# A gated feed-forward stage: its products in two scaled float16 parts, and a store for each batch

## The reference, cut to what matters

```python
x = x + tanh(g_xattn[0]) * L0_xattn(layernorm(x), ctx_2048, mask)      # stage A
x = x + tanh(g_ffn[0])   * L0_ffn(layernorm(x), w_up, w_down)          # stage B
x = x + tanh(g_xattn[1]) * L1_xattn(layernorm(x), ctx_2048)            # stage C
x = x + tanh(g_ffn[1])   * L1_ffn(layernorm(x), w1, w2, w3)            # stage D
# L1_ffn, x: float32 [4, 512, 512], w1, w2: [1408, 512], w3: [512, 1408]
w1, w2, w3 = nf4_roundtrip(w1), nf4_roundtrip(w2), nf4_roundtrip(w3)
a = einsum('bsd,fd->bsf', x, w1)
b = einsum('bsd,fd->bsf', x, w2)
h = silu(a) * b
return einsum('bsf,df->bsd', h, w3)
```

## Time and profile before

| | us |
|---|---|
| median of 3 runs | 1945.01 (1943.62 to 1948.37) |
| profiled execution | 1953.13 |
| its span, first to last instruction | 1951.3 |
| TensorE busy in the span | 1709.4 |
| VectorE busy | 1279.7 |
| ScalarE busy | 788.8 |
| GpSimd busy | 849.4 |

### The profile page before, as it was taken

The page is one execution under the profiler, slowest core; times in us unless marked ns, Lnnn a source line. Parts: engine busy times, 40 slices in busy tenths (PEclk is TensorE's granted clock), DMA queues, the critical chain, the costliest instruction groups (busy, mean ns, idle before and its releaser), DMA issues. The chain is left out here.

```text
span 1951.3 us, 24011 instructions
## 1 busy us (share of the span) xinstructions
PE 1709.4 (88%) x8134; PEld 863.4 (44%) x8134; DVE 1279.7 (66%) x1681; ACT 788.8 (40%) x1291; POOL 849.4 (44%) x383
## 2 busy tenths in 40 slices
PE   5999999993566767999999999999999967989996
PEld 2444444442444544444444444444444324434443
DVE  3668989856987776776766766666766113455453
ACT  1111212112455541566666665666666543111010
POOL 0022222112543434587778776778877740000000
PEclk9999999996888875999999999999999886999998
DMA  8031212302000016244444444444443020000002
GB/s 326 8 103 35 68 68 68 127 30 88 1 1 0 0 49 148 56 107 107 106 107 107 107 107 108 107 107 107 99 98 85 1 89 1 1 0 0 0 0 86
DMA packets 83552, 137.20 MB, mean 70 GB/s; under 512 B 16606, under 2 KB 53490, under 8 KB 82678
## 3 DMA queue, kind: packets, MB, share of 16 engines
q1 hardware_dynamic: 83446, 135.84, 25.4%
HBM read 70.73 MB, written 8.66 MB: 41 GB/s over the span
## 5 line engine op out<-in xcount | busy, mean ns | idle before, releaser
L1261 DVE TENSOR_REDUCE c_piece_max<-c_unit 128x1 f32<-128x804 f32 x512 | 485.2, 985 | 238.8 <-PE c_unit L1399 236.1
L1357 ACT ACTIVATE c_prob<-c_scores 128x512 f32<-128x512 f32 (+1 forms) x832 | 473.8, 597 | 270.4 <-PE c_scores L1416 257.3
L1196 POOL TENSOR_TENSOR c_prob_sum<-c_prob_sum,c_prob 128x2048 f32<-128x2048 f32 x96 | 439.5, 4578 | 13.2 <-ACT c_prob L1357 7.4
L1416 PE MATMUL c_scores<-c_queries,c_keys 98*128 98x512 f32 (+1 forms) x832 | 356.7, 445 | 30.6 <-ACT c_prob L1357 15.5
L1399 PE MATMUL c_unit<-c_khigh,c_qdiag 128*128 128x402 f32 x1024 | 304.4, 382 | 22.3 <-DMA c_qdiag<-c_qhigh 11.2
L1399 PEld LDWEIGHTS c_unit<-c_khigh,c_qdiag 128*128 128x128 f32 x1024 | 187.7, 199 | 153.3 <-DVE c_piece_max L1261 92.2
L1416 PEld LDWEIGHTS c_scores<-c_queries,c_keys 98*128 98x128 f32 (+1 forms) x832 | 153.3, 187 | 199.8 <-ACT c_prob L1357 136.8
L1425 PE MATMUL c_out<-c_prob,c_VT 128*32 128x512 f32 (+1 forms) x1664 | 222.3, 614 | 0.0
L525 PE MATMUL a_S<-a_ctxT,a_xnT 128*128 128x401 f32 x512 | 188.8, 513 | 7.2 <-ACT a_prob L490 3.9
L555 PE MATMUL a_o<-a_ctx,a_probT 128*128 128x512 f32 (+1 forms) x416 | 181.2, 592 | 0.0
L1713 PE MATMUL d_o<-d_w3T,d_h 128*128 128x512 bf16 x528 | 126.7, 392 | 12.3 <-DVE d_h L1620 12.3
(11 more groups left out here) (203 smaller groups left out, 2126.6 us busy)
## 6 DMA issues: line engine op xcount, KB each, us to landing
c_keys<-c_khigh SPq DMA_DIRECT2D x128, 200.2 KB, 3.0
c_k<-in_keys SPq DMA_DIRECT2D x16, 801.0 KB, 6.0
c_keys<-c_k SPq DMA_DIRECT2D x64, 200.2 KB, 3.0
a_ctx<-in_ctx SPq DMA_DIRECT2D x12, 1024.0 KB, 5.5
c_VT<-in_values SPq DMA_DIRECT2D x16, 768.0 KB
a_ctxT<-in_ctxT SPq DMA_DIRECT2D x12, 802.0 KB, 4.8
c_queries<-c_qhigh SPq DMA_DIRECT2D x128, 64.0 KB, 2.7
a_weights<-in_L_ffn_weight SPq DMA_DIRECT2D x3, 1408.0 KB, 13.5
```

The costliest lines, as they stand in the source:

```text
L1196: nc.gpsimd.tensor_tensor(psum4[:], a[:], prob[(j * MC + c) % RING][:], ALU.add).then_inc(sums_taken, 2 if i == 1 else 1)
L1261: nc.vector.tensor_reduce(piece_max[j % 2][:, k // 2, k % 2:k % 2 + 1], U[bank(unit)][:, :, 0:PIECE], axis=AX.XY, op=ALU.max).then_inc(uni ...
L1357: nc.scalar.activation(prob[(j * MC + c) % RING][0:w, h, :], STp[h % 2][0:w, :], ACT.Exp, scale=SCALE).then_inc(exp_done, 1)
L1416: nc.tensor.matmul(STp[h % 2][0:w, :], K[p][:, h, c * P:c * P + w].bitcast(F32R), Q[p][:, h, :].bitcast(F32R), start=True, stop=True).then ...
```

## The change

The hidden products are multiplied by a scale and cut into two float16 parts instead of three bfloat16 parts. The multiplication by the scale goes into the instruction that multiplies silu by the second product. The scale is found at run time from the largest absolute weight: two reductions over the loaded weights, a transpose of the result on TensorE, a reduction, a small matmul that spreads the two values over all partitions, and a few small operations that give the scale and a gate divided by it. The down projection has two matmuls for each tile instead of three, and the addition to x uses the new gate. The four stores leave the fifth block, which is gone, and go into stage D's SyncE stream: each waits for the four additions of its batch.

```diff
+        hids = [sb(f"d_hid{j}", [P, S]) for j in range(3)]
+        hp = [sb(f"d_h{n}", [P, FC, S], F16) for n in ("hi", "lo")]
-        hid = sb("d_hid", [P, S])
-        hrest = sb("d_hrest", [P, S])
-        hp = [sb(f"d_h{n}", [P, FC, S], BF16) for n in range(3)]
+        HALF_RANGE = 2.0 ** 14
...
             for k in range(3):
                 sp.dma_start(wr[k][:], weights_dram[k]).then_inc(w_loaded[k], 16)
+            for b in range(B):
+                sp.wait_ge(x_added, ST + (b + 1) * ST)
+                sp.dma_start(out_dram[b].rearrange("(t p) d -> p t d", p=P), X[:, b * ST:(b + 1) * ST, :]).then_inc(stored, 16)
+            sp.wait_ge(stored, 16 * B)
...
             pool.memset(nhalf[:], -0.5).then_inc(consts_ready, 1)
-            pool.wait_ge(consts_ready, 1)
+            pool.memset(ones2[:], 1.0).then_inc(consts_ready, 1)
+            pool.wait_ge(consts_ready, 2)
...
-                nc.vector.tensor_tensor(hid[:], silu[f % 2][:], U[slot(ST + f)][:, 1, :], ALU.mult).then_inc(unit_read, 1)
+                hid = hids[f % 2 if f < FC - 1 else 2]
+                nc.vector.scalar_tensor_tensor(hid[:], silu[f % 2][:], hscale[:], U[slot(ST + f)][:, 1, :], ALU.mult, ALU.mult).then_inc(unit_read, 1)
                 dve.wait_ge(unit_read, 2 + n + 1)
                 steps.link(nc.vector.tensor_copy(hp[0][:, f, :], hid[:]))
-                steps.link(nc.vector.tensor_tensor(hrest[:], hid[:], hp[0][:, f, :], ALU.subtract))
-                steps.link(nc.vector.tensor_copy(hp[1][:, f, :], hrest[:]))
-                nc.vector.tensor_tensor(hp[2][:, f, :], hrest[:], hp[1][:, f, :], ALU.subtract).then_inc(h_ready, 1)
+                nc.vector.tensor_tensor(hp[1][:, f, :], hid[:], hp[0][:, f, :], ALU.subtract).then_inc(h_ready, 1)
                 steps.close()
 
+            def hidden_scale():
+                steps = Steps(dve, scale_steps)
+                for k in range(2):
+                    dve.wait_ge(w_loaded[k], 16)
+                    nc.vector.tensor_reduce(wmax[:, k:k + 1], wr[k][:], axis=AX.X, op=ALU.max, apply_absolute_value=True).then_inc(wmax_ready, 1)
+                dve.wait_ge(wmax_turned, 1)
+                steps.link(nc.vector.tensor_reduce(wtop[:], O[0][0:2, 0:P], axis=AX.X, op=ALU.max))
+                dve.wait_ge(consts_ready, 2)
+                nc.vector.tensor_scalar(wdiag[:], ident[0:2, 0:2], wtop[:], None, ALU.mult).then_inc(wdiag_ready, 1)
+
+            def hidden_scale_spread():
+                steps = Steps(dve, scale_steps, 1, 1)
+                dve.wait_ge(wtops_spread, 1)
+                steps.link(nc.vector.tensor_copy(wtops[:], O[1][:, 0:2]))
+                steps.link(nc.vector.tensor_tensor(hbound[:, 0:1], wtops[:, 0:1], wtops[:, 1:2], ALU.mult))
+                steps.link(nc.vector.tensor_scalar(hbound[:, 1:2], hbound[:, 0:1], float(D) * D / HALF_RANGE, 1e-30, ALU.mult, ALU.max))
+                steps.did(nc.vector.reciprocal(hscale[:], hbound[:, 1:2]))
+                steps.did(nc.vector.tensor_scalar(hgate[:], hbound[:, 1:2], gates[:, 3:4], None, ALU.mult))
+                steps.settle()
+
             layernorm(0)
+            hidden_scale()
             rest_of_x(0)
+            hidden_scale_spread()
...
-                    nc.vector.scalar_tensor_tensor(x, O[t][:], gates[:, 3:4], x, ALU.mult, ALU.add).then_inc(x_added, 1)
+                    nc.vector.scalar_tensor_tensor(x, O[t][:], hgate[:], x, ALU.mult, ALU.add).then_inc(x_added, 1)
...
+            pe.wait_ge(wmax_ready, 2)
+            nc.tensor.transpose(O[0][0:2, 0:P], wmax[:], ident[:]).then_inc(wmax_turned, 1)
             turn_x(0)
+            pe.wait_ge(wdiag_ready, 1)
+            nc.tensor.matmul(O[1][:, 0:2], ones2[:], wdiag[:], start=True, stop=True).then_inc(wtops_spread, 1)
             up(0, 0)
...
-                        for part in range(3):
+                        for part in range(2):
                             last = nc.tensor.matmul(O[t][:], hp[part][:, f, t * P:(t + 1) * P], w3T[:, f, :],
-                                                    start=f == 0 and part == 0, stop=f == FC - 1 and part == 2)
+                                                    start=f == 0 and part == 0, stop=f == FC - 1 and part == 1)
...
-            ffn_1(nc, shared, weights)
-        with nc.Block() as block:
-            @block.sync
-            def _(sp):
-                for b in range(B):
-                    sp.dma_start(out[b].rearrange("(t p) d -> p t d", p=P), X[:, b * ST:(b + 1) * ST, :]).then_inc(stored, 16)
-                sp.wait_ge(stored, 16 * B)
+            ffn_1(nc, shared, weights, out)
```

More of the change, by code:

```diff
@@ L1498, in _, with ffn_1 @@
             every_slot(pe, slot)
-def ffn_1(nc, shared, weights_dram):
+def ffn_1(nc, shared, weights_dram, out_dram):
     X, ident, ident_bf, gates = shared["X"], shared["ident"], shared["ident_bf"], shared["gates"]
@@ L1531, in ffn_1 @@
         silu = [sb(f"d_silu{j}", [P, S]) for j in range(2)]
-        hid = sb("d_hid", [P, S])
-        hrest = sb("d_hrest", [P, S])
-        hp = [sb(f"d_h{n}", [P, FC, S], BF16) for n in range(3)]
+        hids = [sb(f"d_hid{j}", [P, S]) for j in range(3)]
+        hp = [sb(f"d_h{n}", [P, FC, S], F16) for n in ("hi", "lo")]
+        HALF_RANGE = 2.0 ** 14
+        wmax = sb("d_wmax", [P, 2])
+        wtop = sb("d_wtop", [2, 1])
+        wdiag = sb("d_wdiag", [2, 2])
+        ones2 = sb("d_ones", [2, P])
+        wtops = sb("d_wtops", [P, 2])
+        hbound = sb("d_hbound", [P, 2])
+        hscale = sb("d_hscale", [P, 1])
+        hgate = sb("d_hgate", [P, 1])
         U = [ps(f"d_u{j}", [P, 2, 512]) for j in range(2)]
@@ L1549, in ffn_1 @@
         x_added = sem("d_x_added")
+        stored = sem("d_stored")
+        wmax_ready = sem("d_wmax_ready")
+        wmax_turned = sem("d_wmax_turned")
+        wdiag_ready = sem("d_wdiag_ready")
+        wtops_spread = sem("d_wtops_spread")
+        scale_steps = sem("d_scale_steps")
         ln_steps = sem("d_ln_steps")
@@ L1553, in ffn_1 @@
         UNITS = ST + FC
-        LN_STEPS, H_STEPS = ST + MOMENTS, 3
+        LN_STEPS, H_STEPS = ST + MOMENTS, 1
         tiles = [FC, FC, DC]
@@ L1730, in sem @@
             return stack.enter_context(nc.semaphore(name))
-        gates_loaded, gates_ready, ident_ready, id_steps, weights_stored, stored = (
-            sem(n) for n in ("gates_loaded", "gates_ready", "ident_ready", "ident_steps", "weights_stored", "stored"))
+        gates_loaded, gates_ready, ident_ready, id_steps, weights_stored = (
+            sem(n) for n in ("gates_loaded", "gates_ready", "ident_ready", "ident_steps", "weights_stored"))
         shared = dict(X=X, ident=ident, ident_bf=ident_bf, gates=gates, gates_ready=gates_ready, ident_ready=ident_ready,
```

## The result

| | before | after |
|---|---|---|
| median | 1946.69 us (4 runs, 1943.62 to 1948.71) | 1898.42 us (4 runs, 1896.57 to 1902.01) |
| profiled execution | 1953.13 us | 1898.57 us |
| its span | 1951.3 us | 1896.7 us |
| stage D, from the issue of its weight loads to the end | 354.0 us | 299.6 us |

The ratio is 0.9756, with a 95% interval of 0.9735 to 0.9777, which is a gain of 43 to 52 us. The medians differ by 48.3 us, and 48.8 was the predicted sum. As a time, 1896.2 us was forecast and 1898.4 measured; for the profiled execution 1904.3 was forecast and 1898.6 measured. The two profiles differ by more than the medians, 54.6 us, nearly all of it in stage D: its weight loads are issued at 1597.30 us before and at 1597.15 after. Why they differ by more than the medians is the main question that the experiments had to answer.

What follows compares the result with a forecast made beforehand. Stage D was taken as TensorE-bound batches plus a bare tail of stores. TensorE and VectorE 40.9, stores 8.2, scale -0.3 sum to 48.8 us, taking the median 1945.01 to 1896.2 us, range 1892 to 1901.

Steps and rivals of the forecast that it cites:

- The removed matmuls: Stage D down projection: 176 matmuls go, 168 of them on the path at 0.2158 us, 36.3 us gained.
- Rival D: Down matmuls: float16 stationary with bfloat16 moving runs at float32's rate, 90 us more, time 1986; chance 0.02.
- Rival E: Stage D: VectorE becomes the bound, little more than the stores' 8.2 us gained, time 1936; chance 0.01.
- The product chain: VectorE, each group: 1.19 us shorter, 1.86 stays; gains 2.2 before down(0), 1.0 before down(1), 1.4 at the end.
- the wait before down(1): TensorE waiting while layernorm(b+1) stands between hidden(0) and hidden(1): 3.17 us becomes 2.84, 0.33 gained three times.
- Where x is turned: Batch turn: the first cast on ScalarE decides, so these 4.7 us stay, nothing gained or lost.
- The scale: Start of stage D: reductions hidden beside weight loads and transposes, one small transpose on the path; -0.3 us, bounds 0 and -2.
- The stores: End of kernel: 5.3 us follow the last additions instead of 13.5, 8.2 us gained, bounds 4.8 and 8.6.
- Rival B: Tail: the last store lands no quicker than the median one, 45.4 us gained in all, time 1899.6; chance 0.07.
- The clock: TensorE at half clock behind waits: the 7.3 us of losses stay, change 0, bounds +7.3 and -7.
- Rival C: TensorE: 2.84 us of waiting spares the clock, which no longer falls; 56.1 us gained, time 1888.9; chance 0.07.
- rival A: TensorE: the clock falls more often, each fall dear; 42.3 us gained in all, time 1902.7; chance 0.11.

Runs made afterwards that it cites:

- the third matmul: The kernel after with a third down matmul for each tile, reading the low part again, VectorE's chain kept short; 1930.4 us.
- The repeat: The kernel before, unchanged, profiled and timed once more; median 1951.84 us, stage D 346.2 us.
- The long chain: The kernel after with two more VectorE instructions per group between high and low part, still two down matmuls; 1917.1 us.
- the pieces of the layer normalization: The kernel after with the next batch's layer normalization cut into pieces that VectorE does ahead of groups 2 to 6; 1886.7 us.
- parts alone: The kernel after with the four stores put back in a fifth block, keeping the two float16 parts and their scale; 1906.8 us.
- no scale: The kernel after without the reductions and the spreading, with a plain multiplication and the old gate; 1897.1 us.
- the woven turn: The kernel after with TensorE's order at a batch's end changed, turning x's tiles between parts of the last down matmuls; 1891.2 us.

## Why the prediction was right, point by point

**The removed matmuls: right.** 3.45 and 1.73 us in the chain, 0.216 us a matmul with a float16 stationary operand whose load takes 98 ns. Rival D, a mixed pair at the rate of float32, has no trace of it. Rival E, VectorE as the bound, falls with the third matmul: matmuls put back cost 32.3 of their 36.3 us.

**The product chain: the sum right, the split only one of two.** From down(b, 10) to down(b+1, 0) the forecast was 5.40 us and 5.45 are measured (1703.96 to 1709.41). From down(0) to down(1) it was 8.02, and 8.09 are measured (to 1717.50). The chain is 1.93 us and not 1.86, because the multiply with the scale takes 0.75 us: I had taken a quarter of the 2.73 us of four additions, which overlap, for one alone. Only the wait before down(1) of batch 0 was misjudged: 2.19 us are left of it and not 2.84, since there down(0) no longer waits for VectorE: the layer normalization starts 0.8 us ahead of down(0), and 0.2 in the later batches. Where x is turned 4.73 us stay (1694.43 to 1699.16), as said. At the end, from silu to the last addition, 1.35 us went of 1.4.

Without the clock's falls the stretches before the tail are 40.9 us shorter (346.2 - 13.5 against 296.5 - 4.7). Forecast were 40.9 less 0.3 for the scale, 40.6. The split into 36.3 for the matmuls and 4.6 for the chain is another matter. It follows what each takes away when both change, and neither is what it is worth alone: the matmuls 28.3 or 32.4 us, the chain 8.5 or 12.6, by which comes first. The forecast didn't need this, but whoever makes only half of the change does.

**The scale: 0.3 forecast for finding it, none measured.** The reductions take 11.94 us and end at 1615.66. The small transpose moved turn_x(0) from 24.0 to 24.2 us behind the first weight transpose, and the first up matmul didn't move at all.

**The stores: 8.2 forecast, 8.8 measured.** The landing is 4.3 us, not 4.6, and the issue follows the last addition by 0.02 us. Rival B (a landing of 8.0) fell: that median was of four stores issued within 2.1 us of each other, while every store that is issued alone lands in 4.3. The Trainium skill ("DMA: Bandwidth & Descriptors", Measured) has 6.15 us for a load of 1 MB that GpSimd issues. This store, from SyncE's queue and SBUF to DRAM, takes 4.3, and for it the measurement decides.

**The clock: the term that was mis-sized.** I set the clock's change to 0, with 7.3 us before and the same after, and wrote that the 8.1 us between profile and median of before lay "mainly outside this stage". The repeat shows them inside it. In the profiles the clock took 7.8 us before and 3.0 after, so its term was 4.8 and not 0. With the 0.6 that the stores gave beyond their 8.2, and the 0.3 that finding the scale didn't cost, this is why the profiles differ by 54.6 and not by 48.8 us, and why the 1904.3 us for the profiled execution came out 5.7 too high.

For the medians the term is small: 49.7 without falls, 48.3 measured, so a typical execution of before would lose some 1.6 us to the clock, if one of after loses its 3.0. This is only an inference. The timed executions have no trace, the interval of the gain is 8 us wide, and the kernel before has executions in two groups some 8 us apart, so its median depends on how many of either there are. That 48.3 and 48.8 lie so close is in this part luck. Rival C, no falls at all, is true only behind the first matmuls of batch 1; rival A, more falls than before, was not seen.

The Trainium skill ("TensorE: Matmul & The Clock Gate", HAM oscillation) describes a kernel in which each wait between its bursts of matmuls throttles the clock anew. The long chain agrees, with a fall behind each wait of 3.92 us. The kernel before doesn't: behind three waits of 3.0 us the clock fell three times in one execution and not once in the next. After, it fell behind 2.19 us and not behind 2.74. So the length of a wait doesn't settle it alone; what else does, no run here shows.

## What to carry to other kernels

A profile is one execution. Before you subtract two of them, take the half-clock stretches out of both: here that turned 54.6 us into 49.7, and the forecast's sum for TensorE and VectorE then fitted to 0.3 us. Where two parts of a change meet in the same waits, add up only what both do together: alone, the matmuls gave 28 or 32 us and the chain 9 or 13. Where TensorE waits for VectorE's queue, the order of VectorE's work counts as well as its length: the pieces of the layer normalization, which do the same work in other places, took away 7.7 us of waits. A store that ends a kernel is cheap to move: only its last piece can't be hidden.

## What the runs showed of the hardware that I had not expected

- The clock fell 1.1 us after TensorE had begun to work again (1649.57 to 1650.66), and at the same matmul or the one behind it in parts alone, no scale and the woven turn.
- 48 more matmuls inside waits made stage D 4.5 us shorter, since they kept the clock at 2.4 GHz behind these waits.
- Ten executions of the kernel before came in two groups by their clock, four and six: 1943.4 to 1945.8 us at a mean granted clock of 0.936 to 0.938, and 1951.8 to 1954.6 at 0.930 to 0.934.
- A store of 1 MB beside TensorE's full stream costs it nothing: 75.14 against 75.15 us a batch.
